# Row sums of the routed heads from the exponential's accumulator, and new lists of side steps, in a one-core conv, scan and attention kernel

## What is computed

```python
router_in = hidden_states.mean(axis=1)
logits = router_in @ Wr + br
_, top_idx = jax.lax.top_k(logits, K)                 # K = 6 of H = 12 heads
hard = jax.nn.one_hot(top_idx, H).sum(axis=1)
m = (hard + logits - stop_gradient(logits))[:, :, None, None]
q = proj(Wq, bq) * m                                  # k and v likewise
scores = jnp.einsum('bhqd,bhkd->bhqk', q, k) / jnp.sqrt(jnp.float32(D))
probs = jax.nn.softmax(scores, axis=-1)
ctx = jnp.einsum('bhqk,bhkd->bhqd', probs, v)
x = ctx.transpose(0, 2, 1, 3).reshape(B, S, hid) @ Wo + bo + hidden_states
# then a layernorm with ln_g, ln_b; the block's input is added last
```

## Time and profile before

| | |
|---|---|
| median of three runs | 393.08 us (392.85 to 399.09) |
| the profiled execution | 392.09 us, span 390.3 us |
| TensorE, matmul | 359.1 us, 92% of the span |
| TensorE, weight load | 272.0 us, 70% |
| VectorE | 288.5 us, 74% |
| ScalarE | 213.2 us, 55% |
| POOL | 192.1 us, 49% |
| mean granted TensorE clock | 0.988 of 2.4 GHz |

### The profile page before, as it was taken

How to read it: one execution, slowest core, us unless ns; L and a number is a source line. 1 busy time by engine, 2 the same in 40 slices (tenths; PEclk the granted TensorE clock), 3 DMA queues, 4 the chain that set the end, 5 groups by cost and what they waited for, 6 DMA issues and landing times.

```text
span 390.3 us, 7446 instructions
## 1 busy us (share of the span) xinstructions
PE 359.1 (92%) x2593; PEld 272.0 (70%) x2593; DVE 288.5 (74%) x477; ACT 213.2 (55%) x553; POOL 192.1 (49%) x236
## 2 busy tenths in 40 slices
PE   7998969999799989989899999999999999999990
PEld 6878837668496746666767866657587669888770
DVE  5734887999989988899989999999782600553463
ACT  2576447567455654744863777846645341347530
POOL 5222673797388576579665645855362400210021
PEclk9999999999999999999999999999999999999997
DMA  5703999998899999998987997389900000000010
GB/s 116 139 20 106 241 267 254 256 295 231 215 236 262 243 242 266 241 239 229 247 208 210 220 234 187 101 222 259 250 8 3 0 0 2 2 20 2 3 41 20
DMA packets 26238, 61.82 MB, mean 158 GB/s; under 512 B 6935, under 2 KB 10969, under 8 KB 26201
## 3 DMA queue, kind: packets, MB, share of 16 engines
q1 hardware_dynamic: 26201, 61.35, 63.2%
HBM read 57.15 MB, written 4.19 MB: 157 GB/s over the span
## 4 chain that ended last, share of the span: by engine, by line
PE 38%; DVE 13%; DMA 9%; ACT 5%; issue 4%; POOL 3%; POOLq 0%; ACTq 0%; DVEq 0%; SPq 0%
DMA in_rep<-step_rows 7%; DVE state L1063 6%; PE ring L1232 5%; PE ring L1515 4%; DVE drv L1052 3%; PE ring L1521 2%; PE ring L1442 2%; ACT decay L760 2%; PE y_acc L1398 2%; DMA step_rows<-step 2%; PE ring L1425 2%; POOL outp L583 2%; PE ring L1595 1%; PE ring L1532 1%; PE y_acc L1392 1%
## 5 line engine op out<-in xcount | busy, mean ns | idle before, releaser
L583 POOL TENSOR_TENSOR outp<-state,c_rep 128x512 f32<-128x512 f32 x96 | 122.3, 1289 | 60.4 <-DVE state L1063 35.1
L1063 DVE TENSOR_TENSOR_SCAN state<-decay,drv 128x512 f32<-128x512 f32 x96 | 117.2, 1221 | 10.3 <-ACT decay L760 5.9
L760 ACT ACTIVATE decay<-in_rep,a_neg 128x255 f32<-128x255 f32 x192 | 86.8, 503 | 62.6 <-DMA in_rep<-step_rows 49.9
L1232 PEld LDWEIGHTS ring<-ident 128*128 128x128 f32 x726 | 90.9, 193 | 25.4 <-issue 15.3
L1232 PE MATMUL ring<-ident 128*128 128x128 f32 (+1 forms) x726 | 99.6, 282 | 5.6 <-ACT room_h L675 2.8
L1052 DVE TENSOR_TENSOR drv<-in_rep,b_bc 128x512 f32<-128x512 f32 x96 | 66.4, 692 | 10.2 <-PE b_bc L1373 2.0
L598 POOL TENSOR_SCALAR mv<-mv 128x2 f32<-128x2 f32 x16 | 4.6, 288 | 79.1 <-DVE mv L1077 78.5
L1398 PE MATMUL y_acc<-outp,band 128*32 128x256 f32 x192 | 33.7, 609 | 0.0
L1392 PE MATMUL y_acc<-outp,band 128*32 128x256 f32 x192 | 20.2, 391 | 4.1 <-POOL outp L583 4.1
L1521 PE MATMUL ring<-kvw,tT 96*128 96x480 f32 (+1 forms) x52 | 22.9, 567 | 0.0
L1515 PE MATMUL ring<-tT,qw 96*128 96x256 f32 (+1 forms) x88 | 20.7, 380 | 0.9 <-ACT tT L645 0.9
(11 more groups left out here) (339 smaller groups left out, 618.1 us busy)
## 6 DMA issues: line engine op xcount, KB each, us to landing
in_rep<-step_rows SPq DMA_DIRECT2D x96, 512.0 KB, 6.4
c_rep<-c_rows SPq DMA_DIRECT2D x16, 256.0 KB, 6.4
step_rows<-step SPq DMA_DIRECT2D x8, 384.0 KB, 4.9
x_tok<-in_x_dram SPq DMA_DIRECT2D x4, 192.0 KB, 3.6
out_dram<-res SPq DMA_DIRECT2D x4, 192.0 KB, 2.0
...
```

The lines of the kernel that those rows point to most:

```text
L583: g.tensor_tensor(outp[:, u % SLOTS, :], state[:, u % STATE_SLOTS, :], c_rep[:, part, :], ALU.mult).then_inc(S["outp"], 1)
L760: ins = a.activation(decay[:, back, u % DECAY_SLOTS, e, kept], in_rep[:, slot, 0, :].rearrange("p (e l) -> p e l", e=WAYS)[:, e, kept], AC ...
L1063: v.tensor_tensor_scan(state[:, u % STATE_SLOTS, :][:, order], held[:, order], drv[:, :][:, order], 0.0, ALU.mult, ALU.add).then_inc(S["st ...
L1232: t_.matmul(dst[:, 0:wide], ident[:, 0:cols], ident[:, 0:wide], start=True, stop=True)
```

## The change

In the third block, `exp_scores` lets each exponential accumulate its row sums into `den` (two tiles by six heads, 12 columns an image). A new step dn inverts the 12 columns on VectorE (`inv`) and copies them on ScalarE, each repeated over 16 columns (`inv_all`, 192 columns). A new step iv turns them on TensorE with two products into 96 rows by 256 tokens, which ScalarE copies to `inv_den`. `keep_heads` only multiplies, and `weigh_values` runs the value products alone. The wait for the copies of queries, keys and values moves from the scores to the end of step fv. The lists, the banks and the fill products are new throughout. Fill products number 461 in place of 407; 63 in place of 44 belong to steps ahead of slot 0 in TensorE's list, and 67 in place of 70 to its last list; some now stand ahead of a sum of states ("sum.78"). The diff, the lists cut to the lines that are spoken of:

```diff
--- before.py
+++ after.py
@@
-ONES = 15
+ONES = 11
@@
 PE_SIDE = {
-    -1: "z.0 z.1 z.2 d.1 w_out.0 w_pbd.0 conv0.1 conv1.1 conv2.1 w_qk000.0 z.3", 4: "d.2 conv0.2 conv1.2 w_qk001.0 conv2.2 b0.1",
...
-    96: "yT.3 fo.0 t1.1 gT.3 aT.2 o.3 p.2 w.1 tT.3 q0.3 q1.3 q2.3 kv00.3 kv01.3 kv10.3 kv11.3 cx.3 at.3 hT.2 aT.3 p.3 lg.2 fo.1 hT.3 lg.3 wqk.2 wv.2 fq.2 fk.2 fv.2 wqk.3 s0.2 wv.3 t0.2 s1.2 fq.3 fk.3 fv.3 t1.2 s0.3 w.2 t0.3 s1.3 fo.2 t1.3 w.3 fo.3"}
+    -1: "d.1 w_out.0 z.0 w_pbd.0 w_qk000.0 w_qk001.0 w_qk010.0 w_qk011.0 w_qk100.0 w_qk101.0 w_qk110.0 w_qk111.0 w_v.0 w_proj.0 w_f0.0 w_f1.0 conv0.1 conv1.1 conv2.1 w_f2.0 conv0.2 conv1.2 z.1 b0.1",
...
+    70: "fv.0 s0.0", 73: "b1.6 t0.0 s1.0 yT.2", 76: "wqk.1 wv.1 fq.1 gT.2 o.2", 79: "t1.0 b0.7 iv.0 fk.1 fv.1 s0.1 b1.7",
+    82: "w.0 tT.2", 85: "t0.1", 88: "s1.1", 91: "q0.2 q1.2 q2.2 kv00.2 kv01.2 t1.1",
+    96: "yT.3 kv10.2 kv11.2 fo.0 gT.3 o.3 cx.2 tT.3 iv.1 at.2 q0.3 q1.3 aT.2 q2.3 kv00.3 kv01.3 kv10.3 kv11.3 p.2 cx.3 at.3 w.1 aT.3 p.3 fo.1 hT.2 lg.2 hT.3 lg.3 wqk.2 wv.2 fq.2 wqk.3 fk.2 fv.2 s0.2 wv.3 t0.2 s1.2 fq.3 fk.3 t1.2 fv.3 s0.3 iv.2 w.2 t0.3 s1.3 fo.2 t1.3 iv.3 w.3 fo.3"}
 }
 ACT_SIDE = {
-    -1: "z.0 z.1 z.2 d.1 sp.1", 1: "silu.1 w_out.0", 6: "z.3", 7: "d.2 w_qk000.0", 8: "w_qk001.0", 10: "sp.2", 13: "silu.2",
...
+    -1: "w_out.0 z.0 w_qk000.0 d.1 sp.1 w_qk001.0 w_qk010.0 w_qk011.0 w_qk100.0", 0: "w_qk101.0 w_qk110.0 w_qk111.0", 1: "w_v.0",
+    2: "w_proj.0 w_f0.0", 6: "w_f1.0 w_f2.0", 8: "z.1", 9: "silu.1", 11: "z.2", 14: "d.2", 17: "silu.2", 18: "sp.2 z.3",
...
+    96: "t1.1 y.3 kv01.2 kv10.2 yn.3 gT.3 kv11.2 dn.1 cx.2 tn.3 tT.3 iv.1 q0.3 q1.3 aT.2 q2.3 kv00.3 kv01.3 kv10.3 kv11.3 cx.3 aT.3 un.2 hT.2 un.3 hT.3 lg.2 wqk.2 lg.3 wv.2 fq.2 fk.2 fv.2 wqk.3 s0.2 t0.2 wv.3 s1.2 fq.3 fk.3 t1.2 fv.3 dn.2 s0.3 iv.2 t0.3 s1.3 t1.3 dn.3 iv.3"}
 }
 DVE_SIDE = {
-    -1: "z.0 z.1 z.2 d.1 w_out.0 sp.1 w_pbd.0 mx.1 ms.1", 1: "silu.1", 9: "d.2", 10: "sp.2", 12: "mx.2", 13: "silu.2",
-    14: "ms.2", 19: "silu.3 d.3", 20: "z.3", 22: "sp.3", 24: "mx.3", 25: "yT.0 ms.3", 29: "o.0", 34: "d.4", 38: "sp.4",
-    41: "mx.4 ms.4", 47: "d.5", 50: "yT.1 sp.5 mx.5", 51: "at.0 ms.5", 56: "o.1", 58: "p.0 d.6", 61: "sp.6 mx.6 ms.6",
...
+    -1: "w_out.0 w_pbd.0 d.1 sp.1 mx.1 ms.1 z.0", 9: "z.1", 10: "silu.1", 12: "z.2", 16: "d.2", 18: "sp.2 mx.2 silu.2 ms.2 z.3",
+    21: "d.3", 24: "sp.3", 27: "mx.3 silu.3", 28: "ms.3 yT.0", 31: "o.0", 34: "d.4", 37: "sp.4", 40: "mx.4 ms.4", 45: "d.5",
+    49: "yT.1", 53: "o.1", 54: "sp.5 at.0 mx.5", 55: "ms.5", 58: "d.6 sp.6 p.0", 60: "mx.6", 65: "ms.6 at.1", 66: "lg.0",
+    68: "p.1", 69: "d.7", 73: "lg.1", 74: "s0.0 sp.7", 76: "mx.7 ms.7 s1.0 yT.2", 80: "dn.0", 82: "o.2", 85: "s0.1", 86: "w.0",
+    90: "s1.1",
+    96: "dn.1 yT.3 o.3 fo.0 rn.0 at.2 p.2 at.3 w.1 p.3 fo.1 lg.2 lg.3 s0.2 rn.1 s1.2 dn.2 s0.3 w.2 s1.3 fo.2 dn.3 rn.2 w.3 fo.3 rn.3"}
...
 }
@@ -152,7 +153,7 @@
         return [f"conv_{n}"]
     if step in HEAD_STEPS:
         heads = [] if step == "w" else range(int(step[1]), TOPK, 2)
-        return {"s": [f"s{n}{j}" for j in heads], "t": [f"pt{n}{j}" for j in heads], "w": [f"pv{n}", f"pd{n}"]}[step[0]]
+        return {"s": [f"s{n}{j}" for j in heads], "t": [f"pt{n}{j}" for j in heads], "w": [f"pv{n}"]}[step[0]]
     return [f"{step}_{n}"]
 
 
@@ -331,7 +332,9 @@
         rank = sb("rank", [CK, 2])
         gain = sb("gain", [CK, IMG, 2])
         nmax = sb("nmax", [P, PER_ROUND, 2])
-        one_of = sb("one_of", [P, 2, 2, HD])
+        den = sb("den", [P, IMG, 2, TOPK])
+        inv = sb("inv", [P, IMG, 2, TOPK])
+        inv_all = sb("inv_all", [P, 2, TOPK, HD])
 
         gn_banks = [b_bc[0], b_bc[1], drv, y_acc]
         S = {n: sem("s_" + n) for n in (
@@ -339,7 +342,7 @@
             "gn_turned gn_stats gn_agg gn_dev gn_var gn_eps gn_rsqrt gn_bias xn padded z_kept gate_e gate_s conv conv_e taps minus_cb xs0 xs "
             "a_exp raw c_kept step_kept b_there sp_t sp_s sp_l sp_max sp_in sp_exp sp_ln step decay drive state outp y_mm y_ev "
             "stat_y agg_y eps_y rsqrt_y neg_y shift_y norm_y gate_w gate_m gate stat_t agg_t eps_t rsqrt_t neg_t shift_t norm_t ctx_lo a_rec att "
-            "stat_u agg_u eps_u rsqrt_u neg_u shift_u norm_u router_in prob_max prob weighed logits logit_col ties above rank gain sel sel_m "
+            "stat_u agg_u eps_u rsqrt_u neg_u shift_u norm_u router_in prob_max prob weighed logits logit_col ties above rank gain sel sel_m inv inv_all "
             "stat_r agg_r eps_r rsqrt_r norm_r wsel_zero fin"
         ).split()}
         S["outd"] = [sem(f"s_outd{b}") for b in range(IMG)]
@@ -778,8 +781,8 @@
                 if before:
                     fetched(act, "pt%d%d" % before)
                 for q in range(2):
-                    a.activation(prob[:, i, q, :], bank(name)[:, q * L:(q + 1) * L], ACT.Exp,
-                                 bias=nmax[:, i, q:q + 1]).then_inc(S["prob"] if q == 0 else freed(name), 1)
+                    a.activation(prob[:, i, q, :], bank(name)[:, q * L:(q + 1) * L], ACT.Exp, bias=nmax[:, i, q:q + 1],
+                                 accum_out=den[:, n % IMG, q, j:j + 1]).then_inc(S["prob"] if q == 0 else freed(name), 1)
 
             def side(step, n):
                 h, b = n // IMG, n % IMG
@@ -888,6 +891,15 @@
                 elif step in ("t0", "t1"):
                     for j in range(int(step[1]), TOPK, 2):
                         turned_probs(n, j)
+                elif step == "dn":
+                    act.wait_ge(S["inv"], n + 1)
+                    if n:
+                        fetched(act, f"iv_{n - 1}")
+                    a.copy(inv_all[:], inv[:, b, :, :].unsqueeze(3).to_broadcast([P, 2, TOPK, HD])).then_inc(S["inv_all"], 1)
+                elif step == "iv":
+                    if n:
+                        taken(act, f"pv{n - 1}")
+                    evac(name, (inv_den[:], bank(name)[0:CK, 0:L]))
 
             pre_raw(0)
             pre_softplus(0)
@@ -965,9 +977,6 @@
             for c in range(2):
                 turned_stats(3, c)
             collected(1, IMAGES, 2 * IMAGES)
-            for e in range(2):
-                for d in range(2):
-                    v.memset(one_of[:, e, d, :], float(e == d)).then_inc(S["ones"], 1)
             group_deviations(1, others)
             v.memset(cbd[:], 0.0).then_inc(S["ones"], 1)
             v.memset(eps_all[:], KERNEL_EPS).then_inc(S["ones"], 1)
@@ -1141,8 +1150,7 @@
 
                 p = n % IMG
                 dve.wait_ge(S["weighed"], n + 1)
-                v.reciprocal(inv_den[:], bank(f"pd{n}")[0:CK, 0:L]).then_inc(freed(f"pd{n}"), 1)
-                taken(dve, f"pd{n}")
+                taken(dve, f"iv_{n}")
                 v.tensor_tensor(cT[p][0:CK, :], bank(f"pv{n}")[0:CK, 0:L], inv_den[:], ALU.mult).then_inc(freed(f"pv{n}"), 1)
 
             def side(step, n):
@@ -1181,6 +1189,12 @@
                 elif step in ("s0", "s1"):
                     for j in range(int(step[1]), TOPK, 2):
                         row_max(n, j)
+                elif step == "dn":
+                    for j in range(TOPK):
+                        taken(dve, f"s{n}{j}")
+                    if n >= IMG:
+                        dve.wait_ge(S["inv_all"], n - IMG + 1)
+                    v.reciprocal(inv[:, b, :, :], den[:, b, :, :]).then_inc(S["inv"], 1)
                 elif step == "w":
                     keep_heads(n)
                 elif step == "fo":
@@ -1402,10 +1416,6 @@
                 p = n % IMG
                 heads = range(r, TOPK, 2)
                 banks_ = [begin(f"s{n}{j}") for j in heads]
-                if r == 0:
-                    fill_in(f"s0.{n}", banks_[0])
-                    for w in "qkv":
-                        taken(pe, f"f{w}_{n}")
                 for q in range(2):
                     for j, b_ in zip(heads, banks_):
                         rows = slice(2 * HD * (j // 2), 2 * HD * (j // 2 + 1))
@@ -1429,20 +1439,16 @@
             def weigh_values(n):
                 p = n % IMG
                 begin(f"pv{n}")
-                begin(f"pd{n}")
-                fill_in(f"w.{n}", bank(f"pd{n}"))
                 for j in range(TOPK):
                     taken(pe, f"pt{n}{j}")
                 for r in range(2):
                     for kt in range(2):
-                        for dst in ("pv", "pd"):
-                            for j in range(r, TOPK, 2):
-                                at = 2 * HD * (j // 2)
-                                held = fv[p][:, kt, j, :] if dst == "pv" else one_of[:, r, :, :].rearrange("p e d -> p (e d)")
-                                ins = t_.matmul(bank(f"{dst}{n}")[at:at + 2 * HD, 0:L], held, probT[:, r, j // 2, kt * L:(kt + 1) * L],
-                                                start=(r == 0 and kt == 0), stop=(r == 1 and kt == 1))
-                            if r == 0 and kt == 1:
-                                done(ins)
+                        for j in range(r, TOPK, 2):
```

(13 more changed lines are left out.)

10 lines of the change are left out of this document (5 added, 5 removed), and 58 rows, old and new, of tables (ACT_SIDE, DVE_SIDE, FILLERS, PE_SIDE).

## The result

The changed kernel takes 405.58 us (median of 4, 402.74 to 406.94), the kernel before 395.61 on the same chip (median of 4). The ratio is 1.028, with an interval of 1.022 to 1.034: slower, and outside the forecast's range of 385 to 402. The profiled execution of after took 404.85 us with a span of 403.1, so it is 12.8 us longer than the one of before. By the ratio the loss is some 11 us; the rest of these 12.8 is scatter between executions.

A forecast was written before the change was run, and what follows sets the result against it. It took VectorE's work and waits to bound the loop and TensorE's work the tail: 392.1 for the profiled execution, +2.2 for the loop and +0.7 for the tail gave 395.0 us, range 385 to 402.

The forecast's parts named there:

- VectorE's work: Loop: row maxima 2.1, two gates 0.5 and small inversion 0.3 come in, the 1.75 reciprocal goes out: +1.2 us.
- POOL's and SyncE's moved steps: Loop: input rows queue behind SP's late write; POOL's product waits at slots 17 and 53, its outputs covered by four states.
- The opening: Before slot 0: more fill and weights' products delay the first sum, weight copies delay early slots: +1.8 us, bounds 0 and 4.
- Step transfers: Loop: scans' step sizes finish later for slots 24 and 60, +1.7 and +1.5 us; the wait of index 4 shrinks, -2.0.
- B products: Loop: VectorE's wait for TensorE's B products before slot 90 goes as that list empties: -2.0 us, bounds -2.0 and 0.
- The tail: Last scan to last output product: TensorE -0.3, reciprocal -1.8, inverse +0.9, reads +0.7, scores +1.2: +0.7 us, bounds -3 to +4.
- The sums' part: Tail, TensorE: removed ones products save 5.4 us for images 1 to 3, turning the inverses adds 1.35.
- The inverse's chain: Tail, image 3: copy 0.4 and turn 0.45 stand before the weighing: +0.9 us on the path, bounds 0 and 1.2.
- The scores behind the values: Tail, images 2 and 3: TensorE waits for ScalarE's copy in the value step, 0.6 each: +1.2 us, bounds 0 and 1.5.
- TensorE's sum: Tail: moved steps 9.9 in and 4.5 out, inverses 1.35, removed products -5.4, fill -1.6: -0.3 us.
- The slower rival: Loop: fill products and the opening make TensorE the bound, +7.0 us of its work: 401 us, chance 0.17.
- The faster rival: Image 3's chain sets the tail (-2.4) and the loop loses its named waits (-6.7): 383 us, chance 0.17.

The follow-up runs named there:

- C in time and eight buffers: The changed kernel with seven of SyncE's repeats of C at their earlier slots of before and eight product buffers instead of six: 400.3 us, ratio 1.014.
- the faster kernel: New sums under the lists of the kernel before, with the wait for query, key and value copies back in the scores: 391.07 us, ratio 0.989.
- lists alone: Body of the kernel before, with its ones products and large reciprocal, under the changed kernel's lists, banks and fill products: 412.44 us, ratio 1.047.

## Why the prediction was wrong

It said 395.0 and was 10.6 us under the median. Taken as last scan and tail, it forecast +2.2 and +0.7 us; they are +10.2 and +2.7. The 10.2 are the opening 2.3, work that came in 1.1, collisions 5.2 and idle time of VectorE 1.6.

- **VectorE's work, +1.2: the step that failed.** The work itself is about right: three row maxima 1.9, gates, the small inversions 0.4 in place of 1.7. But the prediction took every side step that stays at its old duration, as part of 43 us. They are 5.2 us longer, by collisions with POOL, which the trace of before already showed: the same step at a mean of 955 ns in the loop and 655 ns at its shortest (the line below: shortest, median and longest in ns). Letting POOL keep pace, with C in time and eight buffers, takes back 6.4 of the loop's 7.9.
- **POOL's and SyncE's moved steps.** The prediction named POOL's wait at its softplus product (7.1 us before, 13.0 after) and priced it at nothing, covered by four states. The cover holds for the scans (they wait 1.2 us for POOL, 0.9 before). What no term held is what a late POOL does to VectorE. And it counted SyncE's step transfers alone; C's repeats, two of them issued behind the slot that needs them (c1.4 at 56 for slot 54, c0.7 at 86 for 84), were passed over.
- **The opening, +1.8.** The first scan is 2.3 us late and the first sum starts at 64.63 us, where 65 was forecast. By slot 9 the scans are 0.2 us behind the kernel before. So in the changed kernel it came back whole and the loss grew behind it; under the old lists it costs 2%.
- **Step transfers, +1.7, +1.5, -2.0, and B products, -2.0.** Waits for decay fell from 5.9 to 3.9 us in all, and the large ones before slots 24 and 60 did not come: VectorE was late itself. The 2.0 us for B are gone, as said.
- **The tail, +0.7.** The sums' part holds: TensorE -4.1 us by the earlier trace rows and the faster kernel's tail, 3.3 of it without fill, with -5.4 + 1.35 forecast. The reciprocal of the earlier trace rows is gone, and 0.06 us after the weighing the multiplication runs. A read makes the exponentials' pitch 0.45 us (0.36 before), 0.09 where 0.11 was taken. The inverse's chain is the forecast +0.9 (copy 390.89, products 391.38, weighing 391.96, below). The scores behind the values came as forecast, too: TensorE idles 0.8 us ahead of those of images 2 and 3 each, while ScalarE copies the values: 1.6 for the forecast 1.2 (one line below); with the wait left in the scores (lists alone) it is 1.5, so the new order costs this, not the moved wait. The term that was mis-sized is TensorE's sum, +1.8 us (87.03 to 88.87) for the forecast -0.3. The fill behind the last scan falls by 0.6 us (150 matmuls in 21.36 us, 140 in 20.79), not by 1.6; the sums give 0.75 less than forecast; the moved steps add 5.7, not 5.4. Two of the six heads turned, and the sum that were counted out, still run behind the last scan, 301.54 to 303.86.
- **The slower rival** came nearest in time (401) and had the wrong cause. TensorE is busy for 233.24 us of the loop, as before, and without fill neither loop is clearly faster (1.025 for 1.028, 0.995 for 1).
- **The faster rival** (383) falls with what stood for it: the loop's waits stayed, and TensorE's load in the tail is no slack. The tail goes with TensorE's matmul time in four kernels (82.9, 87.0, 88.9 and 92.6 us of matmul in 87.7, 91.4, 94.1 and 99.3). By the Trainium skill (Trainium Kernel Development and Optimization, Performance Expectations), which takes the weight loads' share instead, the after's 72.66 us of loads in 94.08 would leave 21 us of slack; the rows don't bear this out, since the faster kernel's tail lost 3.7 us with 4.1 of TensorE's work.

The softplus step in before, then the scores, the reads and the inverse's chain in the tail of after:

```profile
L1032 DVE SCALAR_TENSOR_TENSOR spl<-spe,spl x8: 655/672/2262, 29.4 to 238.0; 96x512 f32<-96x512 f32 x8
```

```profile
378.85 0.45 PE L1422 MATMUL y_acc<-fk,fq 32*128 32x256 f32 x1 [0.80 <-issue]
...
381.17 0.46 ACT L784 ACTIVATE prob<-y_acc,nmax 128x256 f32<-128x256 f32 x1
381.53 0.20 ACT L784 ACTIVATION_READ_ACCUMULATOR prob<-y_acc,nmax 128x1 f32 x1
381.62 0.47 ACT L784 ACTIVATE prob<-ring,nmax 128x256 f32<-128x256 f32 x1
...
390.89 0.35 ACT L898 COPY inv_all<-inv 128x192 f32<-128x192 f32 x1
391.38 0.65 PE L1616 MATMUL ring<-ident,inv_all 128*96 128x128 f32 x4 [1.07 <-ACT inv_all L898]
391.96 1.93 PE L1448 MATMUL ring<-room_c,fv 128*32 128x256 f32 x24
```
